# One order of an attention period for another: own scores first, cross values in bursts of one, one and three groups

## The reference, cut to what matters

```
h1 = ln(x);  x = attn(h1, h1, q1, k1, v1, o1) + x          # own attention,   keys: 100
h2 = ln(x);  x = attn(h2, context, q2, k2, v2, o2) + x     # cross attention, keys: 361
h3 = ln(x);  a, g = split(h3 @ ff_w1 + ff_b1)
out = a * gelu(g) @ ff_w2 + ff_b2 + x
attn: softmax(q k^T / 4) v for each head, heads joined, @ wo + bo
```

## Time and profile before

| what | value |
|---|---|
| median of 3 runs | 1357.21 us (1355.14 to 1361.05) |
| the profiled execution, its own time | 1353.17 us |
| its span, first to last instruction | 1351.3 us |
| granted TensorE clock, mean over the span | 0.991 |
| PE busy over the span | 96% |
| DVE / ACT / POOL busy over the span | 61% / 50% / 28% |
| the 29 periods | 187.7 to 929.3 us, 25.57 us each |
| SP's DMA issues in a period without `load_w1` | 33 |

### The profile page before, as it was taken

The page is one execution under the profiler, slowest core; times in us unless marked ns, Lnnn a source line. Parts: engine busy times, 40 slices in busy tenths (PEclk is TensorE's granted clock), DMA queues, the critical chain, the costliest instruction groups (busy, mean ns, idle before and its releaser), DMA issues. The chain is left out here.

```text
span 1351.3 us, 35359 instructions
## 1 busy us (share of the span) xinstructions
PE 1294.8 (96%) x13364; PEld 1202.7 (89%) x13364; DVE 824.2 (61%) x1728; ACT 681.8 (50%) x1558; POOL 381.4 (28%) x545
## 2 busy tenths in 40 slices
PE   5999789999999999999999999999899999999999
PEld 4999678898898899889898898888689999999999
DVE  5555377777777777777777777777664324252521
ACT  4664345565565565565566566565554231313131
POOL 5421212212212212212212212222176243333331
PEclk8999799999999999999999999999999999999999
DMA  4677455445445455445544444443202101010000
GB/s 124 230 256 228 157 152 156 122 131 161 123 127 159 148 146 161 154 141 153 162 127 141 147 127 138 149 128 95 64 24 74 49 2 49 0 49 0 24 1 25
DMA packets 121669, 155.60 MB, mean 115 GB/s; under 512 B 25012, under 2 KB 115372, under 8 KB 121516
## 3 DMA queue, kind: packets, MB, share of 16 engines
q1 hardware_dynamic: 121516, 153.52, 37.3%
HBM read 62.98 MB, written 28.93 MB: 68 GB/s over the span
## 5 line engine op out<-in xcount | busy, mean ns | idle before, releaser
L1363 ACT ACTIVATE probs<-expin 120x400 f32<-120x400 f32 (+2 forms) x640 | 314.4, 505 | 165.5 <-PE expin L702 108.2
L1037 DVE TENSOR_REDUCE neg_max<-score 100x2 f32<-100x722 f32 x320 | 290.1, 907 | 62.1 <-PE score L676 49.4
L702 PE MATMUL expin<-qs,ks 128*120 128x200 f32 (+2 forms) x1280 | 236.1, 275 | 14.2 <-DMA qs<-max_parts 7.9
L702 PEld LDWEIGHTS expin<-qs,ks 128*120 128x120 f32 (+2 forms) x1280 | 191.9, 179 | 33.3 <-DMA qs<-max_parts 17.5
L676 PE MATMUL score<-ks,qs 128*100 128x362 f32 x640 | 165.5, 340 | 5.6 <-DVE neg_max L1037 4.2
L2427 DVE SCALAR_TENSOR_TENSOR hidden<-ps_a,b_cols,gelu 128x320 f32<-128x320 f32 x100 | 55.1, 551 | 165.1 <-PE ps_a L2351 165.1
L1550 POOL TENSOR_TENSOR var_eps<-mv,eps 100x1 f32<-100x1 f32 x32 | 6.1, 190 | 419.5 <-DVE mv L1105 419.5
L2589 POOL TENSOR_TENSOR hid_lo<-hidden,hid_hi 128x320 fp32r<-128x320 f32 x100 | 87.9, 879 | 122.4 <-ACT hid_hi L2497 122.2
L2509 ACT ACTIVATE gelu<-ps_g,b_cols 128x320 f32<-128x320 f32 x100 | 52.7, 527 | 136.9 <-PE ps_g L2351 136.9
L125 DVE TENSOR_REDUCE neg_max<-score 100x10 f32<-100x1000 f32 x62 | 74.4, 1200 | 54.2 <-PE score L118 54.2
L1570 POOL TENSOR_TENSOR ctx_hi<-ctx_raw,one 128x724 fp32r<-128x724 f32 x32 | 44.6, 1393 | 192.0 <-issue 177.6
(11 more groups left out here) (201 smaller groups left out, 2960.9 us busy)
## 6 DMA issues: line engine op xcount, KB each, us to landing
ks<-kc_parts SPq DMA_DIRECT2D x192, 181.0 KB, 3.0
qk_dram<-qk_parts SPq DMA_DIRECT2D x32, 500.0 KB, 5.2
qs<-q_parts SPq DMA_DIRECT2D x192, 75.0 KB
ks<-qk_dram SPq DMA_DIRECT2D x96, 125.0 KB
ctx_raw<-in_ctxT SPq DMA_DIRECT2D x64, 180.5 KB
ks<-kc_parts SPq DMA_DIRECT2D x96, 90.5 KB, 2.2
qs<-qk_dram SPq DMA_DIRECT2D x64, 125.0 KB
v_dram<-v_rows SPq DMA_DIRECT2D x32, 132.8 KB
```

The lines of the kernel that those rows point to most:

```text
L702: mm = pe.matmul(dst, ks[a][u][:, c, j0:j0 + n], qs[a][u][:, :, q_slot(c) if a == 2 else c, :], start=True, stop=True)
L1037: ins = nc.vector.tensor_reduce(dst, src, AX_X, ALU.max, negate=True)
L1363: nc.scalar.activation(probs[e % NPT][0:n, :], expin[e % 2][0:n, 0:HG * N], ACT.Exp, scale=SCALE)\
```

## The change

Only orders change; no call is added or removed, and no wait is changed inside a call. Because `work_jobs` changes, so does which job shares a PSUM buffer with which.

- **PE.** The period opens with `self_scores(f, 0)`, ahead of `scores_for_exp(1, c, 0, 0)`; `project_kc(c, 0)` comes one `scores_for_exp` earlier. The two `turn_outputs(1, c, ...)` stand together, `project_kc(c, 1)`, `turn_heads(1, c)` and `project_out(1, c)` come earlier, `project_kc(c, 2)` comes later, `turn_max(1, f)` comes after the first cross `times_v`. The five cross `times_v`, a burst of three (groups 0, 1, 2) and a burst of two (3, 4) before, become group 0 alone between `turn_heads(1, c)` and `turn_max(1, f)`, group 1 alone between `scores_for_exp(2, x, 3, 1)` and `cross_scores(s, 4)`, and groups 2, 3 and 4 behind `turn_normalised(c)`, followed by `cross_scores(s, 6)`. `project_vc(c, 2)` and `turn_heads(2, x)` change places.
- **SP.** The period opens with `load_qkv1(e)`, then context and x; `place_max(1, f)` comes behind `place_kc(c, 0)`; `place_kc(c, 1)` comes behind `place_max(2, s)` instead of ahead of `place_q2(c)`.
- **DVE, ACT, POOL.** Their lists follow PE's new order; `result(x)` comes ahead of `max_low(2, s)` on DVE, and on POOL `split_context(f)` ahead of `second_residual(c)`.

```diff
--- before.py
+++ after.py
@@ -41,9 +41,9 @@
 
 
 def work_jobs(x, s, c, f):
-    order = [("KC", c, 0), ("OX1", c, 0), ("MT1", f, 0), ("OX1", c, 1), ("KC", c, 1), ("OT1", c, 0), ("KC", c, 2),
-             ("O1", c, 0), ("VC", c, 0), ("T2", c, 0), ("Q2", c, 0), ("OX2", x, 0), ("VC", c, 1), ("OX2", x, 1),
-             ("QT", c, 0), ("OT2", x, 0), ("VC", c, 2), ("O2", x, 0), ("MT2", s, 0)]
+    order = [("KC", c, 0), ("OX1", c, 0), ("OX1", c, 1), ("KC", c, 1), ("OT1", c, 0), ("MT1", f, 0), ("O1", c, 0),
+             ("KC", c, 2), ("VC", c, 0), ("T2", c, 0), ("Q2", c, 0), ("OX2", x, 0), ("VC", c, 1), ("OX2", x, 1),
+             ("QT", c, 0), ("VC", c, 2), ("OT2", x, 0), ("O2", x, 0), ("MT2", s, 0)]
     return [job for job in order if job[1] is not None]
 
 
@@ -536,14 +536,14 @@
                     .then_inc(w1_landed, 16)
 
             def period(x, s, c, f, e):
+                load_qkv1(e)
+                load_context(f)
                 load_x(f)
+                place_kc(c, 0)
                 place_max(1, f)
-                load_context(f)
-                load_qkv1(e)
-                place_kc(c, 0)
-                place_kc(c, 1)
                 place_q2(c)
                 place_max(2, s)
+                place_kc(c, 1)
                 store_x2(x)
                 place_kc(c, 2)
 
@@ -950,11 +950,11 @@
                 project_out(2, 31)
 
             def period(x, s, c, f):
+                self_scores(f, 0)
                 scores_for_exp(1, c, 0, 0)
-                self_scores(f, 0)
                 scores_for_exp(1, c, 1, 0)
+                project_kc(c, 0)
                 scores_for_exp(1, c, 2, 0)
-                project_kc(c, 0)
                 scores_for_exp(1, c, 3, 0)
                 self_scores(f, 1)
                 scores_for_exp(1, c, 4, 0)
@@ -967,38 +967,38 @@
                 cross_scores(s, 0)
                 scores_for_exp(2, x, 0, 1)
                 turn_outputs(1, c, 0)
-                turn_max(1, f)
+                turn_outputs(1, c, 1)
                 scores_for_exp(2, x, 0, 2)
-                turn_outputs(1, c, 1)
+                project_kc(c, 1)
                 scores_for_exp(2, x, 1, 0)
                 cross_scores(s, 1)
                 scores_for_exp(2, x, 1, 1)
-                project_kc(c, 1)
+                turn_heads(1, c)
+                times_v(2, x, 0)
+                turn_max(1, f)
                 scores_for_exp(2, x, 1, 2)
                 cross_scores(s, 2)
                 scores_for_exp(2, x, 2, 0)
-                turn_heads(1, c)
-                project_kc(c, 2)
+                project_out(1, c)
                 scores_for_exp(2, x, 2, 1)
                 cross_scores(s, 3)
                 scores_for_exp(2, x, 2, 2)
-                project_out(1, c)
+                project_kc(c, 2)
                 scores_for_exp(2, x, 3, 0)
+                scores_for_exp(2, x, 3, 1)
+                times_v(2, x, 1)
                 cross_scores(s, 4)
-                scores_for_exp(2, x, 3, 1)
-                project_vc(c, 0)
                 scores_for_exp(2, x, 3, 2)
                 scores_for_exp(2, x, 4, 0)
+                project_vc(c, 0)
+                scores_for_exp(2, x, 4, 1)
                 cross_scores(s, 5)
-                times_v(2, x, 0)
-                times_v(2, x, 1)
-                times_v(2, x, 2)
-                scores_for_exp(2, x, 4, 1)
-                cross_scores(s, 6)
                 scores_for_exp(2, x, 4, 2)
                 turn_normalised(c)
+                times_v(2, x, 2)
                 times_v(2, x, 3)
                 times_v(2, x, 4)
+                cross_scores(s, 6)
                 project_q2(c)
                 turn_outputs(2, x, 0)
                 cross_scores(s, 7)
@@ -1006,8 +1006,8 @@
                 turn_outputs(2, x, 1)
                 turn_q2(c)
                 cross_scores(s, 8)
+                project_vc(c, 2)
                 turn_heads(2, x)
-                project_vc(c, 2)
                 cross_scores(s, 9)
                 project_out(2, x)
                 turn_max(2, s)
@@ -1259,20 +1259,20 @@
                 kc_low(c, 0)
                 maximum(2, s, 0)
                 divide(1, c, 0)
-                max_low(1, f)
+                divide(1, c, 1)
                 maximum(2, s, 1)
-                divide(1, c, 1)
-                maximum(2, s, 2)
                 kc_low(c, 1)
                 features_low("OT1", c)
+                maximum(2, s, 2)
+                second_input(c)
                 maximum(2, s, 3)
+                max_low(1, f)
+                normalise(c)
+                maximum(2, s, 4)
+                maximum(2, s, 5)
                 kc_low(c, 2)
-                maximum(2, s, 4)
-                second_input(c)
-                maximum(2, s, 5)
-                normalise(c)
+                features_low("T2", c)
                 maximum(2, s, 6)
-                features_low("T2", c)
                 divide(2, x, 0)
                 maximum(2, s, 7)
                 divide(2, x, 1)
@@ -1280,8 +1280,8 @@
                 q2_low(c)
                 features_low("OT2", x)
                 maximum(2, s, 9)
+                result(x)
                 max_low(2, s)
-                result(x)
 
             nc.vector.memset(attn[:, :], 0.0).then_inc(attn_cleared, 1)
             for u in range(2):
@@ -1504,16 +1504,15 @@
                 copy_product(1, c)
                 exponential(2, x, 0, 0)
                 exponential(2, x, 0, 1)
-                max_high(1, f)
                 exponential(2, x, 0, 2)
                 exponential(2, x, 1, 0)
+                kc_high(c, 1)
+                heads_high(1, c)
                 exponential(2, x, 1, 1)
                 exponential(2, x, 1, 2)
-                kc_high(c, 1)
+                max_high(1, f)
                 exponential(2, x, 2, 0)
-                heads_high(1, c)
                 exponential(2, x, 2, 1)
-                kc_high(c, 2)
                 exponential(2, x, 2, 2)
                 exponential(2, x, 3, 0)
                 exponential(2, x, 3, 1)
@@ -1521,6 +1520,7 @@
                 exponential(2, x, 4, 0)
                 exponential(2, x, 4, 1)
                 exponential(2, x, 4, 2)
+                kc_high(c, 2)
                 features_high("T2", c)
                 copy_product(2, x)
                 copy_vc(c, 0)
@@ -1618,8 +1618,8 @@
                 x, s, c, f = roles(p)
                 inverse_deviation(c)
                 first_residual(f)
+                split_context(f)
                 second_residual(c)
-                split_context(f)
             run_out()
     return w1_raw, x2_stored
 
```

## The result

The changed kernel takes **1364.66 us** (median of 9 runs, 1360.62 to 1367.36), against 1357.21 us before (median of 9): +7.45 us. The ratio of the two is 1.0056, with a 95% interval of 1.0038 to 1.0075. The change makes the kernel slower by about half a per cent. The forecast was 1366.5 us; it holds as a number, and that is luck: two of its steps were wrong, and they nearly cancelled.

A forecast was written before the change was run, and what follows sets the result against it. PE's own list bounds the time (busy 728.4 of 741.6 us in the 29 periods). Stretches of +0.25 and +0.07 give +0.32 us a period, +9.3 us over 29: 1366.5 us against the median, range 1356 to 1374.

The forecast's parts named there:

- Second stretch, the heads: PE, project_vc(c, 2) to next project_kc(c, 0): project_out(2, x) newly waits 0.38 us for ACT's copy; stretch 4.53 us, +0.07.
- One of the signs that I gave: Profile after: an idle gap of some 0.3 us ahead of project_out(2, x), released by ACT's copy, in every period.
- Second stretch, the context: SP's load_context and load_x, wanted by POOL late in the period: moving them costs 0; PE's wait for the context goes.
- First stretch: PE, project_kc(c, 0) to project_vc(c, 2): turn_heads leaves -0.26, a scores_for_exp enters +0.20, one burst more +0.31; sum +0.25 us.
- the sum of neighbours: PE's first stretch: costs from other changed neighbouring calls cancel to 0, bounds -0.15 to +0.15 us a period.
- The maximum: PE's 7.9 us of waits for SP's cross maximum stay despite moving place_kc(c, 1): 0, bounds -7.9 to +3 us.
- The own stacks first: SP's load_qkv1(e) at the period's head costs 0, since the load is wanted a whole period later.
- 2: Both PE waits go, the single group costs no more than one inside a burst: 1343.5 us, chance 0.07.
- 3: Dense middle: cross_scores(s, 4) or (s, 5) waits for a maximum behind second_input or normalise on DVE: 1375.2 us, chance 0.15.
- 4: Own stacks wait for the last own times_v, holding SP's head and place_q2: +3 us, 1369.5 us, chance 0.08.

The follow-up runs named there:

- Experiment 9: Changed kernel with SP's x and context loads first and POOL's split before first_residual, then turn_heads(2, x) and project_vc(c, 2) swapped back: 1361.27 us, ratio 1.0045.
- experiments 1 and 2: Changed kernel with load_x(f) back at the head of SP's period, 1355.41 us; changed kernel with POOL's split_context(f) ahead of first_residual(f), 1355.46 us.
- experiments 7 and 8: One cross times_v burst more: in the changed kernel with x, context and split moved first, 1366.00 us; in the kernel before, 1360.74 us.
- experiment 10: Kernel before with only place_kc(c, 1) moved behind place_max(2, s) on SP: 1354.46 us, ratio 0.9994.
- experiment 6: Changed kernel with x, context and split moved first, and times_v(2, x, 1) moved into the last burst, one burst less: 1365.04 us, ratio 1.0069.
- experiment 3: Changed kernel's orders on PE, DVE, ACT and POOL with SP's order of the kernel before: 1528.46 us, ratio 1.1285.

## Why the prediction was right, and where it was wrong

**The sum.** Forecast +9.3 us; +7.45 measured. In periods 1 to 28 of the two profiles, start to start:

| term, us a period | forecast | measured |
|---|---|---|
| `project_kc(c, 0)` to `project_vc(c, 2)`, without the wait for the maximum | +0.25 | -0.03 (20.80 to 20.78) |
| the wait for the maximum in it | 0 | -0.14 (0.30 to 0.16) |
| `project_vc(c, 2)` to `project_kc(c, 0)` | +0.07 | +0.43 (4.46 to 4.89) |
| sum | +0.32 | +0.27 |

**Second stretch, the heads: right.** The wait that I said would take the place of the wait for the context is there in every period: 1.07 us from `turn_heads(2, x)` to `project_out(2, x)`, and 4.56 us for the stretch in the undisturbed periods, against my 4.53. One of the signs that I gave is missing all the same: the profile lists no idle gap ahead of `project_out(2, x)`, because the row of `cross_scores(s, 9)` covers the wait. It shows in the starts and as 0.30 us more of busy time. Experiment 9 shows that the two waits stand in for one another.

**Second stretch, the context: wrong, and the larger error.** The step that failed is one sentence: "`load_context` and `load_x` are wanted by POOL late in the period: 0". It was argued from when SP issues them and not from when they land, and it left out that x is wanted by `first_residual`, which stands ahead of the split. x is issued 9 us later, behind the own stacks, and lands some 7 us after its issue instead of 2.5, behind the context: at 22 to 24.5 us of the period, where POOL should start the split at 23.5 us at the latest. Price: 4.89 - 4.56 = 0.33 us a period by the profile, 9.2 us; 7.6 us by the medians of experiments 1 and 2.

**First stretch: the burst right, the sum wrong.** One burst more costs 0.26 to 0.29 us (experiments 7 and 8) against my 0.31. The rule that I set beside it, of the Trainium skill's TensorEngine Tiling (Array Packing), section Key Properties, says that a change of tiling mode drains the array; that the bill came per burst agrees with it. The step that failed is "I take 0 for the sum of neighbours and -0.15 to +0.15 as its bounds". It was about -0.3. The timeline of PE in after, around the bursts:

```profile
...
506.92 0.82 PE L738 MATMUL work<-identf,pv 128*100 128x128 f32 x6
507.49 0.44 PE L702 MATMUL expin<-qs,ks 128*121 128x200 f32 x2
507.77 0.35 PE L623 MATMUL work<-ctx_hi,w_c 128*128 128x362 f32 x1
...
508.62 0.36 PE L702 MATMUL expin<-qs,ks 128*120 128x200 f32 x2
508.82 0.49 PE L676 MATMUL score<-ks,qs 128*100 128x362 f32 x2
...
514.41 0.71 PE L725 MATMUL attn<-probs,vc 120*17 120x100 f32 x24
515.06 0.57 PE L676 MATMUL score<-ks,qs 128*100 128x362 f32 x2
515.47 0.57 PE L702 MATMUL expin<-qs,ks 128*121 128x200 f32 x4
...
517.71 1.75 PE L725 MATMUL attn<-probs,vc 120*17 120x100 f32 x72
519.39 0.58 PE L676 MATMUL score<-ks,qs 128*100 128x362 f32 x2
519.80 0.89 PE L593 MATMUL work<-w_q,t_hi_T 128*100 128x320 f32 x5
...
520.97 0.49 PE L738 MATMUL work<-identf,pv 128*100 128x128 f32 x3
...
```

The bursts are as in the earlier trace rows: one group 0.65 (514.41 to 515.06), the call behind it 0.41 instead of 0.33, three groups 1.68. But `project_q2` takes 1.17 (519.80 to 520.97) where it took 1.25 right behind a burst; `cross_scores(s, 8)` takes 0.38 (523.09 to 523.47) instead of 0.47, 0.09 less, of which I had expected 0.06; `scores_for_exp(2, x, 1, 0)` 0.20 (508.62 to 508.82) instead of 0.28, because the two `turn_outputs` stand together (506.92, six transpositions) and slow one follower (507.49 to 507.77, 0.28) instead of two; the three `project_kc` are 0.08 shorter together (medians of the undisturbed periods). These four are -0.33. I had priced what each new neighbour adds, and but for `cross_scores(s, 8)` not looked at what each call loses when its old neighbour goes.

**The maximum.** My 0 stood within what one profile can tell: 8 waits instead of 16 in the changed kernel, 11 in experiment 10, and no time in the runs. Whether moving `place_kc(c, 1)` thins them out a little stays open; what it is worth is under 0.3%. That SP waits ahead of `place_q2` anyway, on which my 0 rested, holds in the profile before, but not in the period of the earlier trace rows, where `place_q2` follows at once:

```profile
...
SPq L84 <- ACT q_parts L1322: 49.8, 27, 5.2
...
```

**The own stacks first.** "Loading the own stacks first is covered" holds for the stacks themselves. What it did was to have x and the context issued behind them, 9 and 5 us later in the period.

**Rivals.** 2, 3 and 4 did not come true. The third, a wait of `cross_scores(s, 4)` for a maximum behind `second_input`, is real: it lies right beside the changed kernel, and the single burst there covers it (experiment 6). The fourth named the right call, `load_qkv1` at the head of SP's list, but looked for the harm in `place_q2` and not in the loads behind it.

**A better version.** With one call moved, either way, the new order equals the kernel before (0.9996 and 1.0004) and does not beat it; no run here beats it.

## What to carry to other kernels

When a DMA is moved in its queue, price its landing and not its issue, and read from a trace how long the transfers that now stand ahead of it take: their bytes alone do not say it (here 0.37 MB of context held x up for 4.7 us, and 0.9 MB of own stacks, which moved almost as fast as they were issued, did not). Follow the landing into the list of the engine that waits for it: what stands behind the waiting call there pays. When calls are reordered on an engine whose prices depend on neighbours, write down old and new cost of every pair, also of the pairs that are broken up. A piece of work that looks expensive may be filling a wait; before taking it out, look at what the next call would wait for.

## What the runs showed of the hardware that was not expected

The rows of x take 2.5 us from issue to landing when nothing large stands just ahead of them in SP's queue, and about 7 us right behind the context, although its two issues take SP only 1 us. The nine DMAs of the own stacks, with more than twice the bytes, have moved 0.7 us after the issue of x. What is slow is the second DMA of the context: its 128 packets (by their order, the last 128 of the context) move with about two in flight, for some 5 us, and 20 of the 100 packets of x wait until it is nearly done, while the other 80 do not. So here a DMA with few packets in flight held up part of the next one. Another shape for that DMA was not tried; it might bring x and the context in earlier without moving any call.

A group of products takes 0.52 us, and each burst of them 0.12 us besides, for bursts of one, two and three groups alike (0.65, 1.16, 1.68); with what the calls ahead of it and behind it lose, one burst more costs 0.26 to 0.29 us.

Where PE waited long, its granted clock fell to 0.50 (1.2 GHz) around or right behind the wait: for 3.4 us at 2.5 us of waiting in the first period of the changed kernel, and for 129 of 912 us in experiment 3, where all but one are 2 to 5 us.
